# Token language-model tower on one core: mask loads as contiguous rows, and the FFN's inner layer stored token by token

## The reference

```python
# 1. tokens: embedding beside a window of 3 over looked-up PCA features, masked
masked = pca_lookup[ids] * mask_f[..., None]            # [B, S, 20]
pca_feat = (sum over t-1, t, t+1 of masked) / maximum(sum of mask_f over t-1, t, t+1, 1)
fused = concatenate([emb[ids], pca_feat @ proj_w + proj_b]) @ fus_w + fus_b
h = layernorm(fused) * ln_g + ln_b
# 2. attention without softmax, 16 heads of 16, on X = layernorm(h)
K = X;  Q = rms(X @ Wq.T) * q_norm_w;  V = rms(X @ Wv.T) * v_norm_w
h = h + einsum('blhd,blhde->blhe', Q, cumsum(einsum('blhd,blhe->blhde', K, V), axis=1))
# 3. FFN, 256 -> 1024 -> 256, on layernorm(h)
def act_quant(x):
    scale = 127.0 / clip(max(abs(x), axis=-1, keepdims=True), 1e-05)
    return clip(round(x * scale), -128, 127) / scale
def bit_linear(x, w):                                   # w is rounded to -1, 0, 1 times its mean size
    return einsum('bsd,hd->bsh', act_quant(x), weight_quant(w))
g = depthwise_conv1d(bit_linear(x, w1))                 # 3 taps along the tokens
h = h + bit_linear(silu(g), w2)
```

## Time and profile before

| | us |
|---|---|
| median of 3 runs | 336.42 |
| lowest and highest run | 331.52, 338.84 |
| the profiled execution | 334.21 |
| its span, first to last instruction | 332.5 |

### The profile page before, as it was taken

The page is one execution under the profiler, slowest core; times in us unless marked ns, Lnnn a source line. Parts: engine busy times, 40 slices in busy tenths (PEclk is TensorE's granted clock), DMA queues, the critical chain, the costliest instruction groups (busy, mean ns, idle before and its releaser), DMA issues.

```text
span 332.5 us, 4869 instructions
## 1 busy us (share of the span) xinstructions
PE 202.2 (61%) x1456; PEld 148.7 (45%) x1456; DVE 209.0 (63%) x556; ACT 146.7 (44%) x282; POOL 109.0 (33%) x225
## 2 busy tenths in 40 slices
PE   2250000728803978879869959967958968557544
PEld 0120000515603756668547647656736747334322
DVE  2440000281797381684996995897996898887771
ACT  1000000004500332685776676577577476585811
POOL 9100000164101414428337336337333243441400
PEclk9985555675765885976986995997996995858855
DMA  5200004601010102112012112113212204001000
GB/s 139 87 19 20 19 19 120 229 0 32 7 25 2 32 19 47 36 32 49 17 34 52 45 35 43 56 25 41 63 36 39 58 21 44 33 16 48 2 32 32
DMA packets 30403, 14.13 MB, mean 43 GB/s; under 512 B 15528, under 2 KB 29994, under 8 KB 30378
## 3 DMA queue, kind: packets, MB, share of 16 engines
q1 hardware_dynamic: 28888, 13.18, 16.8%
q10 hardware_dynamic: 1490, 0.65, 0.7%
HBM read 5.41 MB, written 2.10 MB: 23 GB/s over the span
## 4 chain that ended last, share of the span: by engine, by line
DVE 29%; PE 28%; SPq 23%; issue 9%; DMA 5%; ACT 3%; DVEq 1%; POOL 0%; ACTq 0%
SPq L262 11%; PE PO L748 7%; PE PA L685 5%; SPq L304 5%; SPq L264 3%; PE PY L789 3%; DMA feat<-sd 3%; SPq L281 3%; PE PS L707 3%; PE PO L742 2%; PE PH L763 2%; DVE mx L1130 2%; DVE hid L1123 2%; DMA wv_s<-in_wvT_dram 2%; DVE ST L1065 2%
## 5 line engine op out<-in xcount | busy, mean ns | idle before, releaser
L434 POOL TENSOR_TENSOR hid<-hid,tap 128x508 f32<-128x508 f32 x32 | 40.9, 1280 | 35.8 <-DVE hid L1123 35.8
L763 PE MATMUL PH<-xsT,w1q 128*128 128x256 f16 x256 | 42.4, 294 | 16.1 <-DVE hid L1123 16.1
L535 ACT ACTIVATE hid<-PH,cb_s,cw_x 128x256 f32<-128x256 f32 x64 | 36.0, 562 | 24.3 <-PE PH L763 24.2
L730 PE MATMUL PS<-QP,KM 128*128 128x256 f32 x128 | 36.1, 414 | 6.3 <-DVE ST L1065 4.0
L763 PEld LDWEIGHTS PH<-xsT,w1q 128*128 128x128 f16 x256 | 23.6, 103 | 32.9 <-issue 26.1
L748 PE MATMUL PO<-VD,ST 128*64 128x32 f32 x512 | 35.6, 265 | 0.0
L1123 DVE SCALAR_TENSOR_TENSOR hid<-PH,cw_x,hid 128x254 f32<-128x254 f32 x64 | 30.0, 473 | 8.6 <-ACT tap L538 8.4
L748 PEld LDWEIGHTS PO<-VD,ST 128*64 128x64 f32 x512 | 33.9, 186 | 0.0
L364 POOL TENSOR_SCALAR v<-tn 128x2 f32<-128x2 f32 x8 | 2.3, 293 | 90.2 <-DVE tn L982 90.2
L1130 DVE TENSOR_REDUCE mx<-w_s 128x256 f32<-128x1024 f32 x16 | 30.8, 1926 | 0.4 <-ACT w_s L544 0.4
L730 PEld LDWEIGHTS PS<-QP,KM 128*128 128x128 f32 x128 | 23.9, 204 | 15.4 <-issue 12.7
(11 more groups left out here) (184 smaller groups left out, 414.5 us busy)
## 6 DMA issues: line engine op xcount, KB each, us to landing
QP<-QT SPq DMA_DIRECT2D x32, 64.0 KB, 2.1
VD<-Vn SPq DMA_DIRECT2D x32, 64.0 KB, 2.1
out_dram<-y SPq DMA_DIRECT2D x8, 256.0 KB, 2.2
w_s<-in_w1T_dram SPq DMA_DIRECT2D x1, 1024.0 KB, 6.7
w_s<-in_w2T_dram SPq DMA_DIRECT2D x1, 1024.0 KB, 9.2
ids_b<-in_ids_dram SPq DMA_DIRECT2D x1, 896.0 KB
mask_p<-in_mask_dram SPq DMA_DIRECT2D x4, 203.0 KB
fusw_s<-in_fusw_dram ACTq DMA_DIRECT2D x2, 256.0 KB, 3.9
```

The lines of the kernel that those rows point to most:

```text
L434: nc.gpsimd.tensor_tensor(part, part, tap[:, c % 2, :, :, 0:T - 1], ALU.add).then_inc(tap0_ok, 1)
L535: nc.scalar.activation(hid[:, j, :, :].rearrange("p u t -> p (u t)"), hidps(j), ACT.Identity, bias=cb_s[:, j:j + 1], scale=cw_x[:, j, 1:2])
L730: ins = nc.tensor.matmul(PS[k][:, b * 256:(b + 1) * 256], KM[g % 2][:, (k * U + u) * 2 + b, :, :].rearrange("p r m -> p (r m)"), QP[g % 2] ...
L763: ins = nc.tensor.matmul(hidps(j), w1q[:, k, j * 128:(j + 1) * 128], part[:, s, :, k, :], start=(n == 0), stop=(n == 2 * KC - 1))
```

## The change

1. **Loads.** `mask_p` is no longer loaded into. The mask comes like the ids, on all 128 partitions, into a new tile `mask_b`, in four chunks of four sequences; each load takes one contiguous run of 512 values. DVE multiplies it by `keep` (1 on the first 28 of each 32 partitions, 0 elsewhere) into `mask_p`, which is now one chunk of float32 with its zero columns. wq and wv come after the first chunk; chunks 2 and 3 come just ahead of w1 and w2.
2. **Features.** Four chunks of four sequences in place of 2, 2, 4, 4, 4, each with seven operations in place of six. Chunk 1 stands at the end of iteration 0, chunks 2 and 3 at the end of iteration 1.
3. **Weight sums and ternary weights** stand at the end of iteration 2 in place of 1, on ACT, PE and DVE.
4. **Inner layer.** `sl` and `h8` lie token by token, the eight blocks' values of a token together. Silu writes with a step of eight values, the maximum reads four adjacent values a token, `quantise` takes 64 tokens with all eight blocks, and `widen_hid(g, c)` makes the c-th sequence. `down` waits for each sequence's widening by itself. `silu` waits for all four parts of `quantise` two groups before.

The core of the diff:

```diff
-CHUNKS = ((0, 2), (2, 2), (4, 4), (8, 4), (12, 4))
+CHUNK = 4
-        sl = [t[:, :].rearrange("p (j t) -> p j t", j=NJ) for t in (w1_s, w2_s)]
+        sl = [t[:, :].rearrange("p (t j) -> p t j", j=NJ) for t in (w1_s, w2_s)]
-        h8 = sb("h8", [128, NJ, UT], I8)
+        h8 = sb("h8", [128, UT, NJ], I8)
...
-            for q in range(4):
-                sp.dma_start(mask_p[32 * q:32 * q + 29, 2:B, 1:T + 1], mask[2:B, :].partition_broadcast(29)
-                             ).then_inc(ld_rest, 16)
+            def load_tokens(n):
+                seqs = slice(n * CHUNK, (n + 1) * CHUNK)
+                for dst, src in ((ids_b, ids), (mask_b, mask)):
+                    sp.dma_start(dst[:, seqs, :].rearrange("p b t -> p (b t)"),
+                                 src[seqs, :].rearrange("b t -> (b t)").partition_broadcast(128)
+                                 ).then_inc(ld_ids[n], 16)
...
             def silu(g, c):
                 wait(act, tap0_ok, 4 * g + c + 1)
-                wait(act, hs_ok, 4 * (g - 2) + c + 1)
-                nc.scalar.activation(sl[g % 2][:, 2 * c:2 * c + 2, :].rearrange("p j t -> p (j t)"),
-                                     hid_f[:, c * 512:(c + 1) * 512], ACT.Silu).then_inc(silu_ok, 1)
+                wait(act, hs_ok, 4 * (g - 2) + 4)
+                nc.scalar.activation(sl[g % 2][:, :, 2 * c:2 * c + 2].rearrange("p t j -> p j t"),
+                                     hid_f[:, c * 512:(c + 1) * 512].rearrange("p (j t) -> p j t", j=2), ACT.Silu).then_inc(silu_ok, 1)
...
-                nc.scalar.activation(hq[g % 2][:, 4 * c:4 * c + 4, :, :].rearrange("p j u t -> p (j u t)"),
-                                     h8_f[:, c * 1024:(c + 1) * 1024], ACT.Copy).then_inc(hq_ok, 1)
+                nc.scalar.activation(hq[g % 2][:, :, c, :], h8[:, c * T:(c + 1) * T, :].rearrange("p t j -> p j t"),
+                                     ACT.Copy).then_inc(hq_ok, 1)
...
-                wait(pe, hq_ok, 2 * g + 2)
                 for u in range(U):
+                    wait(pe, hq_ok, 2 * g + u + 1)
...
+                nc.vector.tensor_scalar(mask_p[:, :, 1:T + 1], mask_b[:, seqs, :], keep[:, :], None, ALU.mult
+                                        ).then_inc(f_c, 1)
...
-                nc.vector.tensor_reduce(mx[:, c, :], sl[g % 2][:, 4 * c:4 * c + 4, :].rearrange("p j t -> p t j"),
-                                        AX.X, ALU.max, apply_absolute_value=True).then_inc(mx_c, 1)
+                nc.vector.tensor_reduce(mx[:, c, :], sl[g % 2][:, :, 4 * c:4 * c + 4], AX.X, ALU.max, apply_absolute_value=True).then_inc(mx_c, 1)
...
-                nc.vector.tensor_tensor(h8[:, 2 * c:2 * c + 2, :], sl[g % 2][:, 2 * c:2 * c + 2, :],
-                                        PY[:, None, UT:2 * UT].to_broadcast([128, 2, UT]), ALU.mult
+                toks = slice(c * 64, (c + 1) * 64)
+                nc.vector.tensor_tensor(h8[:, toks, :], sl[g % 2][:, toks, :],
+                                        PY[:, UT:2 * UT][:, toks, None].to_broadcast([128, 64, NJ]), ALU.mult
                                         ).then_inc(hs_ok, 1)
```

More of the change, by code:

```diff
@@ L54, in lm_tower_kernel @@
         ids_b = sb("ids_b", [128, B, T], I32)
-        mask_p = sb("mask_p", [128, B, T + 2], I32)
+        mask_b = sb("mask_b", [128, B, T], I32)
+        mask_p = sb("mask_p", [128, 4, T + 2])
+        keep = sb("keep", [128, 1])
         wlen = sb("wlen", [128, 4, T])
@@ L253, in _ @@
         def _(sp):
-            sp.dma_start(ids_b[:, 0:2, :], ids[0:2, :].partition_broadcast(128)).then_inc(ld_ids, 16)
-            sp.wait_ge(mzero_ok, 1)
-            for q in range(4):
-                sp.dma_start(mask_p[32 * q:32 * q + 29, 0:2, 1:T + 1], mask[0:2, :].partition_broadcast(29)
-                             ).then_inc(ld_ids, 16)
-            sp.dma_start(ids_b[:, 2:B, :], ids[2:B, :].partition_broadcast(128)).then_inc(ld_rest, 16)
-            sp.wait_ge(mzero_ok, 2)
-            for q in range(4):
-                sp.dma_start(mask_p[32 * q:32 * q + 29, 2:B, 1:T + 1], mask[2:B, :].partition_broadcast(29)
-                             ).then_inc(ld_rest, 16)
+            def load_tokens(n):
[4 more added lines that the diff above has]
+                                 ).then_inc(ld_ids[n], 16)
+            load_tokens(0)
             sp.dma_start(wq_s[:, :, :], wqT.rearrange("(k p) n -> p k n", p=128)).then_inc(ld_att, 16)
             sp.dma_start(wv_s[:, :, :], wvT.rearrange("(k p) n -> p k n", p=128)).then_inc(ld_att, 16)
+            load_tokens(1)
             sp.dma_start(vw_b[:, :], vw.partition_broadcast(128)).then_inc(ld_small, 16)
@@ L270, in load_ffn @@
             def load_ffn():
+                load_tokens(2)
+                load_tokens(3)
                 sp.dma_start(w1_s[:, :].rearrange("p (k n) -> p k n", k=KC),
@@ L664, in gram @@
                     wait(pe, tct_ok, 1)
-                wait(pe, f_ok, CHUNK_OF[g] + 1)
+                wait(pe, f_ok, g * U // CHUNK + 1)
                 free_pa(g - 2)
@@ L848, in _ @@
             nc.vector.tensor_scalar(spare[:, :], rowv[:, :], float(V), None, ALU.is_ge).then_inc(row_c, 1)
+            nc.vector.tensor_scalar(keep[:, :], rowv[:, :], float(V), None, ALU.is_lt)
             for n in range(3):
@@ L876, in features @@
[L876 to L881 removed]
+                    dve.wait_ge(sel_c, 2)
@@ L882, in features @@
+                dve.wait_ge(f_c, 6 * n + 5)
+                part = feat[:, n * CHUNK * T:(n + 1) * CHUNK * T].rearrange("p (b t) -> p b t", b=CHUNK)
+                nc.vector.scalar_tensor_tensor(out=part, in0=hits[:, :, 0:T], scalar=pc[:, :],
+                                               in1=hits[:, :, 1:T + 1], op0=ALU.mult, op1=ALU.add
                                                ).then_inc(f_c, 1)
-                dve.wait_ge(f_c, 5 * n + 5)
-                nc.vector.scalar_tensor_tensor(out=part, in0=hits[:, 0:m, 2:T + 2], scalar=pc[:, :],
+                dve.wait_ge(f_c, 6 * n + 6)
@@ L885, in features @@
+                nc.vector.scalar_tensor_tensor(out=part, in0=hits[:, :, 2:T + 2], scalar=pc[:, :],
                                                in1=part, op0=ALU.mult, op1=ALU.add).then_inc(f_ok, 1)
@@ L1228, in _ @@
                     features(1)
+                if i == 1:
                     features(2)
-                if i == 1:
                     features(3)
-                    features(4)
+                if i == 2:
                     ternary_weights()
```

49 lines of the change are left out of this document (21 added, 28 removed).

## The result

| | before | after |
|---|---|---|
| median, us | 336.1 (331.52 to 338.84, 4 runs) | 293.69 (291.54 to 298.03, 4 runs) |
| ratio | | 0.876, 95% interval 0.863 to 0.889 |
| profiled execution, its span | 334.21, 332.5 | 293.25, 291.5 |
| mean granted clock of PE | 0.76 | 0.80 |

What follows compares the result with a forecast made beforehand. The bound was PE's empty 35.4 us wait for wq and wv behind mask loads on SP's queue. Terms 39.1 + 2.0 - 0.4 + 2.7 + 2.5 = 45.9 us, from 334.2 to 288; range 281 to 295, with rivals 277 to 299.

Steps and rivals of the forecast that it cites:

- A: Loads at the start: no wait for wq and wv behind masks, earlier first features; 39.1 us less.
- B: First iteration: one chunk of four sequences of features ahead of products(1) instead of six sequences; 2.0 us less.
- C: Second and third iteration: 4.6 us gained, then 5.0 lost by moving the ternary weights; 0.4 us more.
- D: Steady loop, token by token layout: cheaper second maximum, 0.45 of 0.72 us counting in six iterations; 2.7 us less.
- this sign of being wrong: Steady loop: the prediction is wrong if ACT's idle time ahead of Qsq is gone.
- E: Tail: down's first half waits only for the first widening, 1.1 us, plus 1.4 in two groups before; 2.5 less.
- The rule against the change: Inner layer on ACT: far-step writes cost silu 0.36 us each by 16-byte SBUF lines, widening nothing.
- Backlog: Start: 5.5 MB of loads queue without pause, delaying rows and later chunks; 4 to 8 us back, 294; 10%.
- ACT pays for both steps: Inner layer: widening also pays for its step, taking 1.78 us; 8 us back, 296; 13%.
- PE at its full clock early: First iterations: PE enters at 2.4 GHz without the idle pause; 4 to 6 us less, 283; 12%.
- Still one engine: Start: new loads still run on one DMA engine at 19 GB/s; 13 us more, 347, slower; 2%.

Runs made afterwards that it cites:

- e12: Changed kernel with std_row ahead of spread_v in SP's queue, silu in pairs, and the weights' absolute sums back in iteration 1: 279.92 us.
- e1: Changed kernel with only its loads, features and later ternary weights kept, the inner layer block by block as before: 293.79 us.
- e0: The changed kernel run again, unedited: 293.14 us.
- e2: The kernel before with only the new token by token layout of the inner layer: 332.42 us, ratio 0.991 to 1.000.
- e11: Changed kernel with std_row ahead of spread_v in SP's queue and the old block by block inner layer: 285.86 us.
- e8b: Second run of the changed kernel with std_row ahead of spread_v in SP's queue: 284.62 us.
- e10: Changed kernel with std_row ahead of spread_v in SP's queue and silu written in pairs of adjacent values: 281.95 us.
- e8: Changed kernel with std_row ahead of spread_v in SP's queue: 285.33 us.
- e3: Changed loads, inner layer stored block by block, but quantised by 64 tokens, widened and down split by sequence: 293.54 us.
- e5: Changed kernel with silu writing pairs of adjacent values, in the old queue order: 296.7 us, one run.

## Why the prediction was right, and where its sizes were off

**What bounds it, and A.** Right: the empty wait for wq and wv was the case. A was priced 39.1, the matmul came 37.2 earlier. The 35.4 held; the start was mis-sized. I let features(0) start at 6.0, after 1.04 MB at 261 GB/s. It started at 7.65. What was mis-sized is above all the amount: wq and wv, issued right behind at 1.72 and 2.19, share the engines with the tokens. The stretch of the changed kernel:

```profile
2.00:8.00 6.00, 0.00 (x0) 0.00 (x0) 1.37 (x12) 0.78 (x1) 5.93 (x8) 1.00 0.89 225
```

At 225 GB/s the 1.04 MB would have been in at 6.6 us; with wq and wv it is 1.57 MB, 7.0 us after 2.0, so 9.0 for all of it, and the mask landed between. The chunk of features took 4.9 (4.8 priced), up to `projb_x` at 12.58. That it was the company of wq and wv fits these numbers; no run left them out.

**B.** Right: from L868 at 28.19 to `products(1)` at 32.85 it took 4.7 us, priced 4.8.

**C.** Right with its mechanism. From the keys of group 0 to those of group 1 28.0 us replace 32.9, 4.9 less, with 4.6 priced. From group 1 to 2 25.8 replace 21.0, 4.8 more, with 5.0 priced: the wait for the sums, the ternary weights, and the keys 12 us after `Vn` (75.98 + 0.69 to 88.50). e12 shows that 2.0 of the loss were the wait for the sums, which the prediction had named.

**D.** The one step that failed. Its first half was exact: 1.20 us priced for the maximum, 1.21 measured. The second, that "0.45 of the 0.72 count" in each iteration, gave 2.7 us; measured are -1.1 (before against after), 0.8 (e1 against e0), -0.7 (before against e2) and 0.5 (e11 against e8b): nothing, within 1 us, over five iterations (the forecast for five is 2.3). I had looked for what is late next in one place of one iteration, and counted the tap ahead of the first conv alone. Up to `ssv`, just behind that conv, the 0.45 nearly came: 0.4 an iteration in e8b against e11, 0.3 in e0 against e1. What failed is to take it for a gain at the next keys, for the next conv's tap is late as well, and then PE's matmuls at either clock. On ACT silu also took more than priced, 0.51 us extra in place of 0.36, but that is not the cause in the loop: with silu at 0.75 (e10) it takes 117.5, as in e8b. Ahead of Qsq ACT's idle time is 0.23 us, 0.96 before, so this sign of being wrong nearly showed:

```profile
164.67 0.60 ACT L500 ACTIVATE Qsq<-PA 128x512 f32<-128x512 f32 x1 [0.23 <-PE PA L687]
```

**E.** Its first half was right: down's first half starts at 284.75, ahead of the second widening's end at 285.81.

```profile
284.75 3.21 PE PY L791 x16
```

From the start of the last quantise to the end of down the changed kernel takes 5.8 us, before it was 7.3 (321.63 to 328.93): 1.5 for the 1.1 priced. The second half, 1.4 us from the second maximum in the two groups before, is the part that did not come: two silus stand in a row on the chain there (274.80, 2.03 us), and for each the forecast had 0.36 extra where it was 0.51. At clocks of 0.75 to 0.78 the tail takes 77.4 us with the old layout (e11), 76.2 with the new one (e8), 74.4 with the new one and silu in pairs (e12). By these, some 3 us were there, and 1.2 are left once silu is written with a far step; each number is good to about 1 us. The prediction said that the tail would gain 0.7 more were silu free; e10 says up to 2.7, 1.7 by the estimate above.

**The rule against the change.** The Trainium skill (SBUF — State Buffer, "Door 1: The DMA port swizzle") let me expect that silu pays and widening doesn't, with the measured row of the reduction, 0.36 us, as the price. The runs agree on silu, at 0.51 us, and for writes in pairs, two to a line of 16 bytes, at 0.12, in which silu's far read, 1 KB apart, is contained. On widening they differ a little: bytes with a step of 8 took 1136 ns in place of 1059.

**The rivals.** *Backlog*: no; w1 and w2 are issued by 11 us and the loads are through at 23, as the rate row shows (274, then 2). *ACT pays for both steps*: half; silu more than assumed, widening 0.08 in place of 0.72. It cost a part of E's gain; in the loop e10 shows no cost. *PE at its full clock early*: in the profile after it was, 0.88 from 20 to 35 us (first row), in e1 0.50 (second row). The other executions are as divided: 0.91 in e0 and 0.90 in e8b, 0.50 or 0.51 in e3, e5, e8, e10, e11 and e12:

```profile
20.00:35.00 15.00, 9.14 (x42) 7.03 (x44) 8.01 (x24) 1.15 (x3) 6.58 (x18) 0.88 0.06 14
```

```profile
20.00:35.00 15.00, 11.87 (x40) 8.41 (x39) 7.38 (x21) 1.15 (x3) 6.25 (x16) 0.50 0.05 11
```

The keys of group 0 start at 34.7 there and at 35.4 in e1: 0.7 us, not 4 to 6, for the chain is DVE's from 26.8 to 32.9. This is also why the first stages met the forecast so well: A was 1.9 short; the clock gave 0.7 back, C came out at nothing in place of 0.4 lost, and B 0.2 better, so 0.6 were missing at the keys of group 2. *Still one engine*: no.

**The sum.** 45.9 had been forecast against the profiled execution, 41.0 came: 0.6 missing up to the keys of group 2, 3.8 in the loop (2.7 forecast, -1.1 measured), the rest in the tail. That the total came so near owes something to chance: A's shortfall was made up by the clock, C and B, and the tail differs by up to 3.3 us between executions of one kernel. The own range, 281 to 295, is also not built evenly: downwards its bounds are added up (1 + 2 + 3), upwards they would come to 300.

## What to carry to other kernels

Read the queue that issues DMAs as an engine of its own, in order: here it cost 35 us at the start, where four odd-shaped loads stood ahead of the weights, and up to 7 us in the loop, where eight issues stood between a result and the keys, four of them ready long before. Before counting a faster operation on the chain as a gain, follow the second-longest path to the same wait and to the next one as well; one row's slack is an upper bound. When iterations of one loop differ, look at the granted clock of each before explaining it by the code. And when a layout makes one engine's access dense, ask which engine now writes with the far step, and whether two adjacent values can be written together.
